# Convolution rows turned on TensorE instead of loaded as an image, with the stores moved to SyncE's queue

## What is computed

```
kernel = raw_kernel * _nonoverlap_mask(n)      # 25 x 25, taps at every third row and column, centre 0
lat = conv_general_dilated(x, k, padding='SAME', feature_group_count=ch)
out = lat * x + bias
return out + x                                  # = x * (lat + 1) + bias
```

## Time and profile before

| what | value |
|---|---|
| median of 3 runs | 5305.85 us (5299.35 to 5316.5) |
| profiled execution, its own time | 5310.35 us |
| its span | 5308.6 us |
| TensorE busy over the span | 4693.3 us, 88% |
| VectorE, ScalarE, GpSimd busy | 71%, 65%, 47% |
| mean granted clock of TensorE | 0.933 of 2.4 GHz |
| bytes moved by DMA | 967.20 MB, mean 182 GB/s |

### The profile page before, as it was taken

One profiled execution on the slowest core, in us unless ns is written; L12 is line 12 of the kernel. 1 busy time (PEld: TensorE's weight loads), 2 busy tenths in 40 slices (PEclk: granted clock), 3 DMA queues, 4 the chain that ended last, 5 costly groups with the idle time before them and its releaser, 6 DMA issues.

```text
span 5308.6 us, 117786 instructions
## 1 busy us (share of the span) xinstructions
PE 4693.3 (88%) x39114; PEld 4188.8 (79%) x39114; DVE 3760.7 (71%) x10869; ACT 3451.2 (65%) x7242; POOL 2491.4 (47%) x2605
## 2 busy tenths in 40 slices
PE   5766667369999999999999999999999999999975
PEld 4655556348888888888888888888888888888853
DVE  2333333225788888888888888888888888888884
ACT  0000000037888888888888888888888888888853
POOL 2433323214455555555555555555555555555542
PEclk8877778659999999999999999999999999999985
DMA  9999999625666666666666666666666666666541
GB/s 242 263 273 268 272 263 263 192 78 161 179 168 177 175 172 177 176 177 175 168 176 175 172 176 177 178 173 168 176 176 172 176 175 180 173 168 177 160 111 33
DMA packets 809958, 967.20 MB, mean 182 GB/s; under 512 B 236635, under 2 KB 689684, under 8 KB 797204
## 3 DMA queue, kind: packets, MB, share of 16 engines
q1 hardware_dynamic: 751116, 810.92, 57.0%
q10 hardware_dynamic: 58256, 148.74, 10.9%
HBM read 574.93 MB, written 384.61 MB: 181 GB/s over the span
## 4 chain that ended last, share of the span: by engine, by line
PE 66%; DVE 7%; ACT 3%; issue 3%; DMA 0%; POOL 0%; DVEq 0%; POOLq 0%; SPq 0%
PE ps L1020 11%; PE ps L1045 10%; PE ps L1032 10%; PE ps L1061 6%; PE ps L1060 6%; PE ps L1072 5%; PE ps L1084 5%; PE ps L1110 4%; PE ps L1121 4%; PE ps L1097 3%; PE ps L1132 3%; ACT ps L790 1%; DVE gv L945 1%; ACT spec L785 1%; DVE mean L895 1%
## 5 line engine op out<-in xcount | busy, mean ns | idle before, releaser
L720 POOL TENSOR_SCALAR gv<-gv 96x400 f32<-96x400 f32 (+1 forms) x512 | 599.8, 1171 | 1716.7 <-DVE xn L960 1628.7
L341 PE MATMUL cps<-toep,xin 114*128 114x190 f32 (+2 forms) x3456 | 658.8, 358 | 340.1 <-DVE xo L320 246.2
L341 PEld LDWEIGHTS cps<-toep,xin 114*128 114x128 f32 x3456 | 584.0, 212 | 414.7 <-DVE xo L320 250.2
L320 DVE SCALAR_TENSOR_TENSOR xo<-cps,xo 128x180 f32<-128x180 f32 (+3 forms) x576 | 346.9, 622 | 652.5 <-DMA xo<-in_images 417.7
L1045 PE MATMUL ps<-hid,fa 121*128 121x384 f32 (+1 forms) x2048 | 731.2, 439 | 71.8 <-DVE t L984 59.5
L837 ACT ACTIVATE y<-ps 128x1089 f16<-128x1089 f32 (+1 forms) x512 | 573.0, 1119 | 328.2 <-PE ps L1110 328.2
L1020 PE MATMUL ps<-fb,acol 100*96 100x100 f32 x7936 | 771.0, 250 | 16.4 <-DVE spec L952 14.9
L1020 PEld LDWEIGHTS ps<-fb,acol 100*96 100x96 f32 x7936 | 733.1, 164 | 27.3 <-issue 25.8
L1032 PE MATMUL ps<-w1t,xnt 97*121 97x192 f32 x3200 | 702.5, 330 | 0.7 <-ACT xnt L828 0.7
L1060 PE MATMUL ps<-w2t,spec 97*100 97x96 f32 x3968 | 672.9, 251 | 4.1 <-ACT y L837 4.1
L1061 PE MATMUL ps<-w2t,spec 96*100 96x96 f32 x3968 | 675.6, 252 | 0.0
(11 more groups left out here) (101 smaller groups left out, 9921.4 us busy)
## 6 DMA issues: line engine op xcount, KB each, us to landing
a_d<-arow SPq DMA_DIRECT2D x448, 288.0 KB, 4.0
acol<-a_d SPq DMA_DIRECT2D x192, 600.0 KB
xin<-in_items SPq DMA_DIRECT2D x96, 1008.0 KB
g_d<-mixed SPq DMA_DIRECT2D x256, 300.0 KB
tok<-x_d SPq DMA_DIRECT2D x64, 1134.4 KB
out<-o_sb SPq DMA_DIRECT2D x448, 136.1 KB
xo<-in_images ACTq DMA_DIRECT2D x16, 2970.0 KB, 63.0
x_d<-xo ACTq DMA_DIRECT2D x48, 990.0 KB, 20.9
```

Source lines behind the costliest of these rows:

```text
L341: last = nc.tensor.matmul(ps[m % BANKS][:, (r0 - o0) * GC:(r1 - o0) * GC], xin[g % RING][0:GP, c % CG, xr, q, :], toep[e % 2][0:GP, c, at ...
L720: nc.gpsimd.tensor_scalar(v, v, 0.0, None, ALU.max).then_inc(v_cut, 1)
```

## The change

`in_images` and its loads go away. TensorE makes the image rows itself: behind each x block's matmul, the same x block, still the stationary operand, is multiplied by a unit matrix of 114 columns (`nc.tensor.transpose`), which turns it into the result's layout, in a second PSUM bank. ScalarE copies that bank into `xo`, so an item now goes TensorE, ScalarE (`copied`), VectorE (`gated`). The eight PSUM banks serve as four pairs, so TensorE waits for the item four before (`DEEP`) and not eight. The stores, which ScalarE's queue issued, are issued by SyncE between its loads of `xin`.

The core of the diff:

```diff
-BANKS = 8
+DEEP = 4
...
         @block.sync
...
+            def store(t, n):
+                e, k = t // 2, t % 2
+                r0, r1 = parts(k)[n]
+                if on_dve(t, n):
+                    sp.wait_ge(biased[1], 1)
+                else:
+                    sp.wait_ge(biased[0], biases_before(t, n))
+                for h in range(2):
+                    nr, ys = image_rows(k, e, h, r0, r1)
+                    sp.dma_start(x1[e].rearrange("b (y x) c -> b y (x c)", y=R)[:, ys, :],
+                                 xo[k][e % 2][h * B:(h + 1) * B, r0:r0 + nr, :, :]
+                                 .rearrange("p r x c -> p r (x c)")).then_inc(stored[k][e % 2], 16)
...
                     if k == 0 and g == 3 and e + 1 < E:
                         load_taps(e + 1)
+                    if g == 1 and t >= 2 and k == 0:
+                        store(t - 2, 2)
+                    if g >= 4 and t:
+                        store(t - 1, g - 4)
+            store(PASSES - 2, 2)
+            for n in range(len(parts(1))):
+                store(PASSES - 1, n)
...
         @block.scalar
...
-            def load_images(t):
...
-            act.wait_ge(blank, 2)
-            for t in range(4):
-                load_images(t)
-            for t in range(PASSES):
-                for n in range(len(parts(t % 2))):
-                    store(t, n)
-                if t >= 1 and t + 3 < PASSES:
-                    load_images(t + 3)
...
+            act.dma_start(unit[:, :], identity[0:GP, 0:GP]).then_inc(unit_in, 16)
+            for t in range(PASSES):
                 e, k = t // 2, t % 2
+                o0, rows, _ = KINDS[k]
                 if e >= 2:
                     act.wait_ge(stored[k][e % 2], 32 * len(parts(k)) * (e // 2))
...
+                for n in range(PER):
+                    m, xr = t * PER + n, n % DIL
+                    cols = len(range(xr, R, DIL))
+                    turned_x = ps[2 * (m % DEEP) + 1][:, o0 * GC:(o0 + rows) * GC]
+                    act.wait_ge(lat_done, m + 1)
+                    nc.scalar.activation(xo[k][e % 2][:, :, xr::DIL, n // DIL],
+                                         turned_x.rearrange("p (r x) -> p r x", r=rows)[:, :, 0:cols],
+                                         ACT.Copy).then_inc(copied, 1)
...
         @block.vector
...
-                dve.wait_ge(image_in[k][e % 2], 32 * (e // 2 + 1))
...
-                    dve.wait_ge(lat_done, m + 1)
+                    dve.wait_ge(copied, m + 1)
...
         @block.tensor
...
-                    if m >= BANKS:
-                        pe.wait_ge(gated, m - BANKS + 1)
+                    if m >= DEEP:
+                        pe.wait_ge(gated, m - DEEP + 1)
...
+                        last = nc.tensor.transpose(ps[2 * (m % DEEP) + 1][:, q * GP:(q + 1) * GP], xb, unit[:, :])
                     last.then_inc(lat_done, 1)
```

More of the change, by code:

```diff
@@ L64, in conv_items @@
     return np.ascontiguousarray(v.transpose(0, 4, 2, 3, 5, 6, 1, 7)).reshape(2, C // CG, GP, CG * DIL * BLK * ITEMS)
-def conv_images(x):
-    return np.ascontiguousarray(x.reshape(B, R, R, E, EC).transpose(3, 0, 1, 2, 4))
 def conv_bands(raw):
@@ L172, in transform_constants, with conv_stage @@
     return {name: np.ascontiguousarray(v.astype(np.float32)) for name, v in out.items()}
-def conv_stage(nc, xh, xi, bands, cb, x1):
+def conv_stage(nc, xh, bands, cb, identity, x1):
     with ExitStack() as ctx:
@@ L190, in conv_stage @@
         cbias = sb("conv_cbias", [128, C])
-        ps = [ctx.enter_context(nc.psum_tensor(f"cps{s}", [128, 512], F32)) for s in range(BANKS)]
+        unit = sb("unit", [GP, GP])
+        ps = [ctx.enter_context(nc.psum_tensor(f"cps{s}", [128, 512], F32)) for s in range(2 * DEEP)]
         cb_in = sem("cb_in")
-        blank = sem("blank")
+        unit_in = sem("unit_in")
+        copied = sem("copied")
         toep_in = [sem(f"toep_in{s}") for s in range(2)]
         x_in = [sem(f"x_in{s}") for s in range(RING)]
-        image_in = [[sem(f"image_in{k}{s}") for s in range(2)] for k in range(2)]
         stored = [[sem(f"stored{k}{s}") for s in range(2)] for k in range(2)]
@@ L251, in _ @@
                         load_taps(e + 1)
+                    if g == 1 and t >= 2 and k == 0:
[5 more added lines that the diff above has]
+                store(PASSES - 1, n)
+            for k in range(2):
+                for s in range(2):
+                    sp.wait_ge(stored[k][s], 32 * len(parts(k)) * E // 2)
         @block.scalar
@@ L254, in _ @@
         def _(act):
-            def load_images(t):
+            act.dma_start(cbias[:, :], cb.rearrange("(a c) -> a c", a=1).broadcast_to([128, C])).then_inc(cb_in, 16)
+            act.dma_start(unit[:, :], identity[0:GP, 0:GP]).then_inc(unit_in, 16)
+            for t in range(PASSES):
                 e, k = t // 2, t % 2
+                o0, rows, _ = KINDS[k]
                 if e >= 2:
                     act.wait_ge(stored[k][e % 2], 32 * len(parts(k)) * (e // 2))
[L259 to L275, removed]
@@ L277, in _ @@
-            act.dma_start(cbias[:, :], cb.rearrange("(a c) -> a c", a=1).broadcast_to([128, C])).then_inc(cb_in, 16)
-            act.wait_ge(blank, 2)
-            for t in range(4):
-                load_images(t)
-            for t in range(PASSES):
-                for n in range(len(parts(t % 2))):
-                    store(t, n)
-                if t >= 1 and t + 3 < PASSES:
-                    load_images(t + 3)
-            for k in range(2):
-                for s in range(2):
-                    act.wait_ge(stored[k][s], 32 * len(parts(k)) * E // 2)
+                for n in range(PER):
[6 more added lines that the diff above has]
+                                         ACT.Copy).then_inc(copied, 1)
@@ L298, in _ @@
         def _(pool):
-            for v in xo[1]:
-                nc.gpsimd.memset(v[B:2 * B, 9, :, :], 0.0).then_inc(blank, 1)
             pool.wait_ge(cb_in, 16)
@@ L316, in _ @@
                     cols = len(range(xr, R, DIL))
-                    lat = ps[m % BANKS][:, 0:rows * GC].rearrange("p (r x) -> p r x", r=rows)[:, :, 0:cols]
+                    lat = ps[2 * (m % DEEP)][:, 0:rows * GC].rearrange("p (r x) -> p r x", r=rows)[:, :, 0:cols]
                     v = xo[k][e % 2][:, :, xr::DIL, n // DIL]
-                    dve.wait_ge(lat_done, m + 1)
+                    dve.wait_ge(copied, m + 1)
                     nc.vector.scalar_tensor_tensor(v, lat, 1.0, v, ALU.add, ALU.mult).then_inc(gated, 1)
@@ L326, in _ @@
         def _(pe):
+            pe.wait_ge(unit_in, 16)
             for t in range(PASSES):
@@ L336, in _ @@
                         pe.wait_ge(x_in[g % RING], LOADS * (g // RING + 1))
-                    if m >= BANKS:
-                        pe.wait_ge(gated, m - BANKS + 1)
+                    if m >= DEEP:
+                        pe.wait_ge(gated, m - DEEP + 1)
                     for i, (q, r0, r1) in enumerate(blocks):
                         at = r0 - GR * q + GR
-                        last = nc.tensor.matmul(ps[m % BANKS][:, (r0 - o0) * GC:(r1 - o0) * GC],
-                                                xin[g % RING][0:GP, c % CG, xr, q, :],
+                        xb = xin[g % RING][0:GP, c % CG, xr, q, :]
+                        last = nc.tensor.matmul(ps[2 * (m % DEEP)][:, (r0 - o0) * GC:(r1 - o0) * GC], xb,
                                                 toep[e % 2][0:GP, c, at * GC:(at + r1 - r0) * GC],
                                                 start=(i == 0), stop=(i == BLK - 1))
+                        last = nc.tensor.transpose(ps[2 * (m % DEEP) + 1][:, q * GP:(q + 1) * GP], xb, unit[:, :])
                     last.then_inc(lat_done, 1)
@@ L1175, in build @@
     g_d = nc.dram_tensor("g_d", [B, S, M, C], F32).ap()
-    conv_stage(nc, p["items"], p["images"], p["bands"], p["cb"], x1)
+    conv_stage(nc, p["items"], p["bands"], p["cb"], p["c_id"], x1)
     mixer_stage(nc, x1, p, a_d, g_d, out)
@@ L1185 @@
     arrays, p = {}, {}
-    for name, a in (("items", conv_items(np.asarray(inputs["x"]))), ("images", conv_images(np.asarray(inputs["x"]))),
-                    ("bands", conv_bands(np.asarray(inputs["L0_conv_raw_kernel"])))):
+    for name, a in (("items", conv_items(np.asarray(inputs["x"]))), ("bands", conv_bands(np.asarray(inputs["L0_conv_raw_kernel"])))):
         arrays[f"in_{name}"] = a
```

## The result

The changed kernel takes 5125.18 us (median of 4 runs, 5108.97 to 5131.13) against 5302.6 us of the kernel before on the same chip. The ratio is 0.9659, with a 95% interval from 0.9641 to 0.9676. Forecast were 5095 us with a range from 5050 to 5170: the direction and the range held, and the forecast was 30 us too low.

A forecast was written before the change was run, and what follows sets the result against it. Transfers, above all image loads, were taken as the bound. Start 14 + TensorE 762 + clock 2 + near misses 10 = 788 us for the matmuls' end, against 998.9, giving 5095 us, range 5050 to 5170.

The forecast's parts named there:

- The bound changes to TensorE, at 762 us: Convolution matmuls: with turns TensorE needs 762 us against 606 us of transfers and becomes the bound; chance 0.66.
- Start, 14 us: Before the first matmul: taps and first x blocks, without images, arrive by 14 us including landing.
- Near misses on SyncE's queue, 10 us: x block loads behind stores on SyncE's queue hold narrowly; 10 us over all passes, ends 0 and 60.
- the clock's term: First stretch of the convolution's matmuls: TensorE runs at half clock, costing 2 us, at most 3.
- The transfers stay the bound (0.22): Rival, convolution: transfers still bound, matmuls end at 840 us, 5150 us in all; break-even rate 252 GB/s; chance 0.22.
- My 317 GB/s for one queue: Convolution's transfers: the 192.0 MB that stay move at 317 GB/s, the rate of stores alone, in 606 us.
- The clock does not rise (0.07): Rival, convolution: turns don't count as work, TensorE at half clock throughout, 5857 us, or 5415 in kind 1 alone; chance 0.07.
- the 3.4 us ahead of the rise: Sign against the clock rival: gapless TensorE work with four turns last, 0.81 us, then granted clock 0.99.
- The chain of an item: Copy, gate and hand-overs per item: 2.2 us, hidden by three items, costed at nothing; rival 5245 us, chance 0.04.

The follow-up runs named there:

- e1_ring4: The changed kernel with four x block buffers instead of three: 5079.36 us, ratio 0.9574 to the kernel before.
- e3_turns_twice: The changed kernel with every turn done twice, the second into the same place: 5259.74 us in one run.
- e8_all: The changed kernel with four x block buffers, SyncE's stores spread singly behind loads, taps moved, unit matrix loaded with 128 rows: 5069.98 us.
- e2_no_turns: The changed kernel without the 1728 turns, ScalarE copying the convolution's bank instead, so the output differs: 5005.34 us, ratio 0.9434.
- e6_deep2: The changed kernel with four x block buffers and two PSUM bank pairs instead of four: 5192.56 us in one run.

## Why the prediction was right, and where its 30 us are

The forecast put the end of the matmuls at 788 us, and it came at 820.7. Term by term:

**The bound changes to TensorE, at 762 us.** Right: the stretch without waits took 761.4 us (e1_ring4) and adding turns lengthened it in full (e3_turns_twice). That the 762 was met so closely is in part luck, as the single prices were off both ways: an item took 1.55 us in kind 0 and 1.08 in kind 1 (e1_ring4), where I had 1.54 and 1.11. In this row group of the changed kernel, kind 1, a turn's slot is 108.61 - 108.51 = 0.10 us:

```profile
108.29 0.39 PE L340 MATMUL cps<-toep,xin 114*128 114x114 f32 x2
108.51 0.26 PE L343 MATMUL cps<-unit,xin 114*128 114x114 f32 x1
108.61 0.39 PE L340 MATMUL cps<-toep,xin 114*128 114x114 f32 x2
```

By the starts of all 1728, it is 0.097 us, where I took 0.112. But the first of the two instructions of a 190-column matmul now takes 0.175 us to the second, where it was 0.161, and for 342 columns 0.302 against 0.287. A turn in front of the second half of such a matmul thus costs about 0.11 in all; one between matmuls of 114 columns, or a second one behind the first (e3_turns_twice), 0.097.

**Start, 14 us.** Wrong by 5: 19.1. I costed the transfers of taps and x blocks and left out the load of the unit matrix, which is new. It has 114 rows, and its completion came in 6 updates of its semaphore, at 17.6 to 19.0 us, while the first x blocks were there at 15.4. With 128 rows TensorE started at 15.60 us and waited for the x blocks (e8_all). So 3.5 of the 5.1 us are the unit matrix, and the other 1.6 the x blocks, which I had at 14.

**Near misses on SyncE's queue, 10 us.** This is the term that was mis-sized: 23.1 us of waits, and 17 us lost to half clock behind them, together 40 us in place of 10 (the half clock at the very start, 2 us, was about right). The step said that a load behind two stores comes after 11.7 us, where 13.3 are allowed. It took 16.6 us. The price of a transfer was not off: from 99.0 to 119.3 us the queue moved 6.13 MB at 302 GB/s. I had counted one pair of stores ahead of the load, but two pairs and three loads are issued within 13 us at the end of a kind 1 pass, 7.2 MB, more than the engines move in that time; and its last part landed 8 us after its first. I had given 60 us as the upper end, which is why the range held. I had also left out that a late load costs twice, once as a wait and once as clock.

**The transfers stay the bound (0.22).** No: DMA share 0.76. Without the turns the same transfers let the stretch end in 679 us (e2_no_turns). My 317 GB/s for one queue gave 606 us; the engines made 305 GB/s while busy, which is 630 us for the same bytes, and the rest of the 679 us is time in which they weren't full.

**The clock does not rise (0.07).** No. In the changed kernel the clock was 1.00 for 95 us at a time with turns in every item, and in e3_turns_twice for 923 us, with six turns of 0.097 us in a kind 1 item of 1.37 us. The Trainium skill ("TensorE: Matmul & The Clock Gate", Part 4, PE-mode transpose) says that transposes don't count for the full level and that it doesn't engage for them. These two traces don't agree for float32 turns between matmuls, which ran at the full level for those 95 and 923 us, and here the measurement decides. They don't show that turns count by themselves, as matmuls stood between all of them; nor did, where 2.6 of the 3.4 us ahead of the rise were other work. What did lower the clock were waits of 2.5 to 4.0 us.

**The chain of an item.** Hidden, as costed, and 1.9 us in kind 0 where I had 2.2 (worked out in e6_deep2). But two sizes in it were off against each other: the hand-overs were shorter, and the copy took longer, 0.79 us for 342 columns where I took 0.44 to 0.49, which gives ScalarE 367 us and not 200 to 260.

```profile
L286 ACT ACTIVATE xo<-cps 128x324 f32<-128x324 f32 x192 | 145.2, 756 | 157.0 <-PE cps L343 157.0
L286 ACT ACTIVATE xo<-cps 128x180 f32<-128x180 f32 x192 | 96.3, 501 | 107.8 <-PE cps L343 107.8
L286 ACT ACTIVATE xo<-cps 128x342 f32<-128x342 f32 x96 | 76.0, 791 | 131.5 <-PE cps L343 131.5
```

Together: 5.1 (start) + 40.2 - 10 (waits and clock) - 2 (of the clock's term, since that is in 761.4) - 0.6 = 32.7 us, the difference between 788 and 820.7.

## What to carry to other kernels

When transfers are the bound, look at each kind of transfer alone: the one that went away moved at two thirds of the rate of the stores, and TensorE could make the same rows for 0.1 us per block. When two streams are put on one queue, add up everything that is issued within the reserve of the tightest buffer, not only the transfer right ahead; the order in which equal bytes are issued was worth 40 us here, and so was one more buffer. Short waits on TensorE cost more than their length, since the clock falls behind them: here 23 us of waits cost 40. With two buffers used in turn, a chain that is too long makes itself felt once in two items.

## What the runs showed of the hardware

- Image loads (rows of 2640 bytes, from DRAM) ran at 204 GB/s with all DMA engines full, stores of rows of the same size at 317 GB/s. Why the loads are slower wasn't tried.
- A float32 turn of 114 columns is one instruction in the trace and takes 0.097 us at full clock, less than half of what the two instructions of a 114-column matmul take (0.22 us).
- A turn between matmuls lengthens the step between the two instructions of the next float32 matmul by 0.014 us, for 190 as for 342 columns; for 114 columns the step stays at 0.112 us. The cause is open.
- ScalarE's copy from PSUM into every 36th element of `xo` took 0.79 us for 342 columns; its copies of 384 columns into adjacent elements in the mixer took 0.49 us. From 180 to 324 columns the copy into `xo` grew by 0.255 us, 1.8 ns a column. Whether the step alone makes the difference wasn't tried.
- The load of the unit matrix with 114 rows completed in 6 updates of its semaphore, the last at 19.0 us; with 128 rows it completed in 16, the last at 14.1 us (e8_all).
